# A one-core audio tower layer: the expert loop's engines hand over in rounds, with one signal per engine and step

## The chip, the cores and the metric

The kernel runs on one NeuronCore of a Trainium2 chip. The metric is device time in microseconds (us), the median over runs. Engines: PE (TensorE, matmuls and transposes), ACT (ScalarE), DVE (VectorE), POOL (GpSimd), SP (SyncE, which here only issues DMAs); the DMA engines move data beside them. Engines wait for each other with semaphores: an instruction may increment one at its end, and another engine waits until the count is reached. "Signal" below means such an increment.

## What is computed

The input is x, 128 x 125 x 64. A depthwise convolution of stride 2 (5 taps) with a group norm and PReLU gives 128 x 63 x 64; a selective state-space block and then a mixture of experts are added to it, each behind a layer norm. The change touches the experts:

```python
xf = x.reshape(-1, D)                       # 8064 tokens of 64
logits = xf @ Wr + br                       # 64 experts
topk_logits, topk_idx = jax.lax.top_k(logits, TOP_K)      # TOP_K = 2
gates = jax.nn.softmax(topk_logits, axis=1)
combine = jnp.zeros((T, E), xf.dtype).at[jnp.arange(T)[:, None], topk_idx].add(gates)
for e in range(E):
    h = jax.nn.relu(xf @ W1[e] + b1[e])     # 64 -> 128
    y = h @ W2[e] + b2[e]                   # 128 -> 64
    out = out + combine[:, e:e + 1] * y
```

All of it is float32.

## The kernel before, in words

The tokens lie as 63 tiles of 128. The first half of the program (to about 380 us) computes convolution and state-space block. Then the routing: DVE finds each token's two experts (`choose`, MAX8 and FIND_INDEX8 per tile), PE counts and ranks them, DVE works out for each token a row in a table sorted by expert. POOL scatters the tokens into this table, `sorted_rows`, with one indirect DMA per tile and choice (L629, 126 of them), and after the experts gathers their results from `expert_out` with 126 more (L650). The 63 tiles are dealt with in three shares (16, 24 and 23 tiles), each with tables of its own; a share's experts need all its scatters, its gathers all its experts' results.

**The expert loop** (about 514 to 778 us) has 80 steps. A step takes two pairs, a pair two tiles of 128 rows, each tile with the weights of one expert. In a step
- PE transposes the rows (`rows_T`, L886, 2 instructions), multiplies by W1 (`hidden`, L897, 8) and by W2 (`outputs`, L910, 8);
- ACT copies the transposes out of PSUM (`xT_copy`, L1165), takes the relu of one half of the hidden values (`relu_A`, L1174, 2), issues a load of rows every second step (L369), and stores the results of a step (`store`, L1183);
- DVE takes the other half's relu (`relu_B`, L1610, 2) and copies the outputs from PSUM into `y_e` (`y_copy`, L1620). Behind each copy it makes two pieces of the gates table (`gates_at`, L1629), and every eighth step adds eight tiles of it (L1637);
- SP loads the weights of a pair (L438) into a ring of 23 places as soon as the copy of the step that used the place is done.

The loop is written out, and each hand-over has a semaphore of its own: `s_rT` (transposes done), `s_rTc` (copied), `s_hid`, `s_reluA`, `s_reluB`, `s_yps` (outputs done), `s_yb` (copied). PE's order in step i is rows_T(i+2), hidden(i+1), outputs(i). All eight PSUM banks are in use; the outputs have one set (banks 6 and 7), so outputs(i) wait for y_copy(i-1). The outputs are computed for 192 columns, of which the last 64 are wanted: the weights lie as W1 (128 columns), W2 (64), bias (1) in a row, and columns 0 to 191 are multiplied.

POOL doesn't run freely in the loop. `keep_pace` makes every second indirect DMA wait until DVE has copied a given step: DMA number d (0 to 251, scatters and gathers together) waits for step (d - 56) * 80 / 153, for even d from 58 to 208. From d = 206 on the gathers are those of the last share, which need all stores. After the loop PE computes the bias part (transposes L942, matmuls L933), ACT and DVE pass it on (L1220, L1665), and DVE weights and adds the gathered rows (L1657, L1659).

DVE's helper `Chain` counts its own instructions on `s_dve`; `link` increments and waits.

## Time and profile before

| | |
|---|---|
| median of 3 runs | 859.83 us (858.7 to 861.21) |
| the profiled execution | 855.41 us |
| its span, first to last instruction | 853.5 us |
| granted TensorE clock, mean over the span | 0.826 of full speed |
| busy, share of the span | PE 60%, DVE 66%, ACT 39%, POOL 70% |
| instructions | 9083 |
| moved by DMA | 85 MB, 100 GB/s over the span |

The profile is one execution, so sums are made against its 855.41. An engine's busy time counts its working instructions; a PE instruction's end is modelled, and PE can be shown as done while the signal of its end is still to come. Releasers are inferred from the records of the semaphores; "remote" and "another core or an unknown queue" mean that no releaser was found, "issue" that the engine waited for nothing that the profile shows. The granted clock is 1.0 at 2.4 GHz and 0.5 at 1.2 GHz.

### The profile page before, as it was taken

To read this page: it belongs to the slowest core of one execution; us is meant where nothing else is said; L and a number is where in the kernel's file an instruction comes from. 1 tells how busy PE (TensorE), PEld (TensorE's weight loads), DVE (VectorE), ACT (ScalarE), POOL (GpSimd) and SP (SyncE) were. 2 spreads that over 40 slices of the span, in tenths; PEclk is the share of its full clock that TensorE was granted. 3 is DMA by queue.
4 is the path that set the end of the run, shared out by engine and by line. 5 is a ranking of instruction groups with operands and counts; after the bars stand their busy time and mean duration, and the time that the engine had idled before them with its cause. 6 is when DMAs were issued, how large, how long until landed. Compare 5 with 4: busy or idle time off the path is not lost.

```text
span 853.5 us, 9083 instructions
## 1 busy us (share of the span) xinstructions
PE 511.2 (60%) x2514; PEld 338.5 (40%) x2520; DVE 565.8 (66%) x1180; ACT 331.1 (39%) x622; POOL 600.2 (70%) x393
## 2 busy tenths in 40 slices
PE   4744245657568566556636767867677768786100
PEld 4733012222122222223323445756566657666100
DVE  1597899999999999997815763445444444332073
ACT  2159856556556655543311412323322332322000
POOL 5895779999999999991364454655555555564674
PEclk9969568797878789986756786999999998999655
DMA  7999950000000000000036013887877877831122
GB/s 247 383 180 123 74 3 0 0 0 0 0 1 0 0 0 0 0 0 0 20 84 161 15 67 110 229 222 211 235 225 209 241 214 208 224 90 47 23 73 62
DMA packets 106605, 84.96 MB, mean 100 GB/s; under 512 B 30464, under 2 KB 90240, under 8 KB 106560
## 3 DMA queue, kind: packets, MB, share of 16 engines
q1 hardware_dynamic: 79312, 54.76, 29.8%
q10 hardware_dynamic: 19184, 21.40, 8.0%
q0 software_dynamic: 8064, 8.27, 4.0%
q8 instruction: 19, 0.31, 0.2%
q14 instruction: 26, 0.21, 0.1%
HBM read 57.22 MB, written 33.49 MB: 106 GB/s over the span
## 4 chain that ended last, share of the span: by engine, by line
POOL 28%; PE 24%; DVE 16%; issue 14%; another core or an unknown queue 11%; ACT 4%; SPq 1%; POOLq 1%; DMA 0%; DVEq 0%; ACTq 0%
POOL x_w L577 14%; POOL w_ring L570 11%; PE ps L910 10%; PE ps L897 5%; POOL xt L650 3%; DVE x_w L1610 2%; DVE x_w L1620 2%; PE ps L675 2%; PE ps L739 1%; PE ps L886 1%; DVE mi L1515 1%; DVE lstat L1297 1%; PE ps L766 1%; PE ps L664 1%
## 5 line engine op out<-in xcount | busy, mean ns | idle before, releaser
L739 PE MATMUL ps<-x_w,ident 128*128 128x512 f32 x252 | 153.8, 770 | 100.7 <-POOL x_w L577 100.7
L629 POOL DMA_INDIRECT sorted_rows<-xp,slot_i x126 | 123.7, 981 | 116.4 <-DVE x_w L1620 35.2
L650 POOL DMA_INDIRECT xt<-expert_out,slot_i x126 | 123.3, 979 | 84.7 <-DVE x_w L1620 42.7
L570 POOL TENSOR_TENSOR w_ring<-xt,bc 128x2016 f32<-128x2016 f32 x32 | 143.4, 4483 | 13.4 <-DVE hh_ring L1426 7.3
L1426 DVE TENSOR_TENSOR_SCAN hh_ring<-ps,w_ring 128x1024 f32<-128x1024 f32 x64 | 147.5, 2305 | 0.1
L577 POOL TENSOR_TENSOR x_w<-hh_ring,bc 128x2016 f32<-128x2016 f32 (+1 forms) x32 | 141.1, 4411 | 1.2 <-PE ps L739 1.2
L739 PEld LDWEIGHTS ps<-x_w,ident 128*128 128x128 f32 x252 | 60.2, 249 | 197.0 <-POOL x_w L577 123.2
L1620 DVE COPY x_w<-ps 128x256 f32<-128x256 f32 x80 | 33.9, 424 | 108.0 <-remote 53.7
L1074 ACT ACTIVATE ps<-dt_t,a_exp 128x1024 f32<-128x1024 f32 x64 | 71.6, 1119 | 64.2 <-DVE hh_ring L1426 64.1
L1068 ACT ACTIVATE ps<-dt_t,a_exp 128x1024 f32<-128x1024 f32 x64 | 71.6, 1119 | 51.0 <-DVE w_ring L1405 51.0
L1165 ACT ACTIVATE x_w<-ps 128x256 f32<-128x256 f32 x80 | 30.8, 385 | 138.7 <-PE ps L886 57.6
L1405 DVE TENSOR_TENSOR w_ring<-ps,w_ring 128x1008 f32<-128x1008 f32 x64 | 78.3, 1223 | 4.1 <-ACT ps L1068 4.1
L1420 DVE SCALAR_TENSOR_TENSOR w_ring<-ps,w_ring 128x1008 f32<-128x1008 f32 x64 | 77.4, 1209 | 0.0
L910 PE MATMUL ps<-dt_t,x_w 128*128 128x192 f32 x280 | 57.2, 346 | 27.2 <-DVE x_w L1620 26.2
L910 PEld LDWEIGHTS ps<-dt_t,x_w 128*128 128x128 f32 x280 | 46.5, 195 | 32.2 <-issue 23.5
L910 PE MATMUL ps<-x_w 128*128 128x192 f32 x224 | 45.5, 345 | 17.6 <-DVE x_w L1620 13.5
L910 PEld LDWEIGHTS ps<-x_w 128*128 128x128 f32 x224 | 37.0, 194 | 21.5 <-issue 13.6
L910 PE MATMUL ps<-bc,x_w 128*128 128x192 f32 x136 | 28.7, 352 | 18.0 <-DVE x_w L1620 17.9
L1610 DVE TENSOR_SCALAR x_w<-ps,dt_t 128x128 f32<-128x128 f32 x70 | 21.5, 346 | 21.1 <-PE ps L897 19.2
L886 PE MATMUL ps<-ident,x_w 128*128 128x128 f32 x160 | 32.0, 285 | 0.4 <-issue 0.4
L910 PEld LDWEIGHTS ps<-bc,x_w 128*128 128x128 f32 x136 | 23.3, 200 | 20.7 <-issue 19.9
L1174 ACT ACTIVATE x_w<-ps,dt_t 128x128 f32<-128x128 f32 x70 | 22.2, 365 | 23.7 <-PE ps L897 20.4
(209 smaller groups left out, 887.9 us busy)
## 6 DMA issues: line engine op xcount, KB each, us to landing
dt_t<-packed SPq DMA_DIRECT2D x140, 96.5 KB
x_w<-packed SPq DMA_DIRECT2D x112, 96.5 KB
x_w<-sorted_rows ACTq DMA_DIRECT2D x40, 256.0 KB
expert_out<-x_w ACTq DMA_DIRECT2D x80, 128.0 KB
sorted_rows<-pad_rows SPq DMA_DIRECT2D x2, 3584.0 KB, 24.1
bc<-packed SPq DMA_DIRECT2D x68, 96.5 KB
packed<-in_L_ffn_W SPq DMA_DIRECT2D x3, 2048.0 KB, 42.0
x_w<-in_x SPq DMA_DIRECT2D x7, 448.0 KB, 8.7
```

What stands on the lines that cost most here:

```text
L570: pool.tensor_tensor(w_buf(k, 2), up3[:, bass.ds(c * DC, DC), 1:S].unsqueeze(1).broadcast_to([P, 2, DC, L]), vec_of(k, 2), ALU.mult).then_ ...
L577: pool.tensor_tensor(hc_buf(k, n), h_buf(k, n), vec_of(N + k, n), ALU.mult).then_inc(s_hcp, n)
L629: pool.indirect_dma_start(out=sorted_rows[h], out_offset=bass.IndirectOffsetOnAxis(ap=slot_i[:, c, l:l + 1], axis=0), in_=xn[:, l, :], in_ ...
L650: pool.indirect_dma_start(out=y[:, l, :], out_offset=None, in_=expert_out[h], in_offset=bass.IndirectOffsetOnAxis(ap=slot_i[:, c, l:l + 1] ...
L739: ins = pe.matmul(ps[:, i, :], ident[:, :], src[:, i * BANK:(i + 1) * BANK], start=(k < 0), stop=(k == (N - 2 if last else N - 1)), skip_g ...
L910: last = pe.matmul(ps[:, 6 + j, t * OUT:(t + 1) * OUT], hT_e[:, i % 2, t, j, :], w_of(n)[:, t, 0:OUT], start=True, stop=True)
L1068: act.activation(banks(6, 2), d, ACT.Tanh, scale=a_exp[:, 2, k:k + 1]).then_inc(s_th, 1)
L1074: act.activation(banks(2 + 2 * (k % 2), 2), d, ACT.Exp, scale=a_exp[:, 1, k:k + 1]).then_inc(s_dA, 1)
L1405: dve.tensor_tensor(wv, body(banks(6, 2)), wv, ALU.mult).then_inc(s_g, 1)
L1420: dve.scalar_tensor_tensor(out=wv, in0=body(dA), scalar=1.0, in1=wv, op0=ALU.add, op1=ALU.mult).then_inc(s_b, 1)
L1426: dve.tensor_tensor_scan(hh_ring[:, k % 4, :], dA, w_ring[:, k % 4, :], 0.0, ALU.mult, ALU.add).then_inc(s_h, 1)
L1620: dve.tensor_copy(y_e[:, i % YRING, 0:m], ps[:, 6:6 + m, 0:2 * OUT].rearrange("p q (t d) -> p q t d", d=OUT)[:, :, :, OUT - C:OUT]).then_i ...
```

## The change

The loop becomes rounds. In round k PE does outputs(k-4), hidden(k-2) and rows_T(k) and then increments one semaphore, `s_pstep`. ACT's round k waits for that and does xT_copy(k) and relu_A(k-2), then `s_astep`; behind it come the load of rows and store(k-5). DVE's round k waits for PE's round k and does relu_B(k-2) and y_copy(k-4), then `s_dstep`; behind it the gates of k-2. PE's round k waits for ACT's and DVE's rounds k-2. There are 84 rounds. The outputs of a step now fill one bank, alternately 6 and 7: four pieces of 128 columns (`OUT = 2 * C`), the last 64 wanted. SP and POOL wait for `s_dstep` where they waited for `s_yb` (`dve_rounds` turns a number of copied steps into one of rounds), and `LAG` grows from 12 to 16, so DMA d waits for step (d - 60) * 80 / 153, for even d from 62 to 212. Outside the loop DVE no longer increments after each instruction of a run of independent ones, only after the last.

```diff
+LAG_H, LATE = 2, 4
...
-OUT = 3 * C
+OUT = 2 * C
...
-LAG = 12
+LAG = 16
...
+def dve_rounds(steps):
+    return steps + LATE - LAG_H
...
                 if n >= WRING:
-                    sp.wait_ge(s_yb, step_of(n - WRING) + 1)
+                    sp.wait_ge(s_dstep, dve_rounds(step_of(n - WRING) + 1))
...
                 if d in STEP_AT:
-                    pool.wait_ge(s_yb, STEP_AT[d])
+                    pool.wait_ge(s_dstep, dve_rounds(STEP_AT[d]))
...
             def outputs(i):
 
-                pe.wait_ge(s_reluA, i + 1)
-                pe.wait_ge(s_reluB, i + 1)
-                if i >= 1:
-                    pe.wait_ge(s_yb, i)
                 for j, n in enumerate(pairs_of(i)):
                     for t in range(2):
-                        last = pe.matmul(ps[:, 6 + j, t * OUT:(t + 1) * OUT], hT_e[:, i % 2, t, j, :],
-                                         w_of(n)[:, t, 0:OUT], start=True, stop=True)
-                last.then_inc(s_yps, 1)
-
-            rows_T(0)
-            rows_T(1)
-            hidden(0)
-            for i in range(STEP0[-1]):
-                if i + 2 < STEP0[-1]:
-                    rows_T(i + 2)
-                if i + 1 < STEP0[-1]:
-                    hidden(i + 1)
-                outputs(i)
+                        last = pe.matmul(ps[:, 6 + i % 2, (2 * j + t) * OUT:(2 * j + t + 1) * OUT], hT_e[:, i % 2, t, j, :],
+                                         w_of(n)[:, t, HID + C - OUT:HID + C], start=True, stop=True)
+                return last
+
+            for k in range(STEP0[-1] + LATE):
+                if k >= LAG_H:
+                    pe.wait_ge(s_astep, k - LAG_H + 1)
+                if k >= LATE:
+                    pe.wait_ge(s_dstep, k - 2 * LAG_H + 1)
+                    last = outputs(k - LATE)
+                if LAG_H <= k < STEP0[-1] + LAG_H:
+                    last = hidden(k - LAG_H)
+                if k < STEP0[-1]:
+                    last = rows_T(k)
+                last.then_inc(s_pstep, 1)
...
+            for k in range(STEP0[-1] + LAG_H):
+                act.wait_ge(s_pstep, k + 1)
+                if k < STEP0[-1]:
+                    last = xT_copy(k)
+                if k >= LAG_H:
+                    last = relu_A(k - LAG_H)
+                last.then_inc(s_astep, 1)
+                if k < STEP0[-1]:
+                    next_rows(k)
+                if k > LATE:
+                    store(k - LATE - 1)
+            for i in range(STEP0[-1] + LAG_H - LATE - 1, STEP0[-1]):
+                store(i)
...
                 for l in range(v.start, v.stop):
-                    dve.max(mx[:, l, :], logits[:, l, :]).then_inc(s_dve, 1)
-                ch.at = ch.at + v.stop - v.start
-                dve.wait_ge(s_dve, ch.at)
+                    last = dve.max(mx[:, l, :], logits[:, l, :])
+                ch.link(last)
...
-            relu_B(0)
-            for i in range(STEP0[-1]):
-                if i + 1 < STEP0[-1]:
-                    relu_B(i + 1)
-                y_copy(i)
+            for k in range(LAG_H, STEP0[-1] + LATE):
+                dve.wait_ge(s_pstep, k + 1)
+                if k < STEP0[-1] + LAG_H:
+                    last = relu_B(k - LAG_H)
+                if k >= LATE:
+                    last = y_copy(k - LATE)
+                last.then_inc(s_dstep, 1)
+                i = k - LAG_H
```

**PE, two steps early in the loop.** `ps` is PSUM, `x_w` the memory with rows, hidden values and some of the weights, `dt_t` other weights; "x3" means three more like it. Before:

```order
L897 MATMUL ps<-x_w 128x128 [waits s_rTc,s_win5,s_win4]
L897 MATMUL ps<-x_w 128x128 x3
L910 MATMUL ps<-x_w 128x192 [waits s_yb,s_reluB,s_reluA]
L910 MATMUL ps<-x_w 128x192 x3
L886 MATMUL ps<-ident,x_w 128x128 [waits s_rows2]
L886 MATMUL ps<-ident,x_w 128x128
L897 MATMUL ps<-x_w 128x128 [waits s_rTc,s_win7,s_win6]
L897 MATMUL ps<-x_w 128x128 x3
```

Now, with `hidden` still L897, `outputs` L906 and the transposes L887:

```order
L906 MATMUL ps<-x_w 128x128 [waits s_dstep,s_astep]
L906 MATMUL ps<-x_w 128x128 x3
L897 MATMUL ps<-x_w 128x128 [waits s_win5,s_win4]
L897 MATMUL ps<-x_w 128x128 x3
L887 MATMUL ps<-ident,x_w 128x128 [waits s_rows2]
L887 MATMUL ps<-ident,x_w 128x128
L906 MATMUL ps<-x_w 128x128 [waits s_dstep,s_astep]
L906 MATMUL ps<-x_w 128x128 x3
```

The outputs stand first in a round and carry all its waits for other engines; hidden waits for its weights alone, and the outputs are 128 columns wide.

**DVE, a step in the loop.** `s_st0` and `s_st1` are the semaphores of the stores that must have landed before a place of `y_e` is written again. Before:

```order
L1620 COPY x_w<-ps 128x256 [waits s_yps,s_st0]
L1629 TENSOR_SCALAR us_lg<-iota_e,top 128x64
L1629 TENSOR_SCALAR hh_ring<-iota_e,top,gate 128x64
L1610 TENSOR_SCALAR x_w<-ps,dt_t 128x128 [waits s_hid]
L1610 TENSOR_SCALAR x_w<-ps,dt_t 128x128
L1620 COPY x_w<-ps 128x256 [waits s_yps,s_st1]
```

Now:

```order
L1595 TENSOR_SCALAR x_w<-ps,dt_t 128x128 [waits s_pstep]
L1595 TENSOR_SCALAR x_w<-ps,dt_t 128x128
L1604 COPY x_w<-ps 128x256 [waits s_st0]
L1612 TENSOR_SCALAR us_lg<-iota_e,top 128x64
L1612 TENSOR_SCALAR hh_ring<-iota_e,top,gate 128x64
L1595 TENSOR_SCALAR x_w<-ps,dt_t 128x128 [waits s_pstep]
```

The two relus and the copy of a round have one wait for PE, ahead of the relus; before, relus and copy had one each. The copy is of a step two before that of the relus; it was one before.

## Rows read from the trace of the kernel before

**Rows 1.** The page, the chain that ended last, by engine.
```profile
POOL 28%; PE 24%; DVE 16%; issue 14%; another core or an unknown queue 11%; ACT 4%; SPq 1%; POOLq 1%; DMA 0%; DVEq 0%; ACTq 0%
```

**Rows 2.** By stretch: PE, PEld, DVE, ACT, POOL busy, clock, DMA share, GB/s.
```profile
560.00:600.00 40.00, 30.57 (x233) 26.25 (x232) 17.97 (x63) 12.44 (x38) 23.65 (x24) 1.00 0.80 223
```

**Rows 3.** Waits, 520 to 780 us: us in total, times, longest.
```profile
ACT x_w L1165 <- PE ps L886: 57.6, 37, 4.3
...
DVE x_w L1620 <- remote: 53.7, 25, 4.5
```

**Rows 4.** Timeline, 630.5 to 638.5: start, us, instructions, [idle before <-releaser].
```profile
630.74 0.42 DVE L1620 COPY x_w<-ps 128x256 f32<-128x256 f32 x1 [2.34 <-remote]
...
631.44 1.01 POOL L629 DMA_INDIRECT sorted_rows<-xp,slot_i  x1 [1.66 <-DVE x_w L1620]
...
632.69 0.38 PE L886 MATMUL ps<-ident,x_w 128*128 128x128 f32 x2
...
633.10 0.39 ACT L1165 ACTIVATE x_w<-ps 128x256 f32<-128x256 f32 x1 [1.49 <-PE ps L886]
...
633.64 1.57 PE L910 MATMUL ps<-x_w 128*128 128x192 f32 x8
...
635.30 0.97 POOL L629 DMA_INDIRECT sorted_rows<-xp,slot_i  x1 [0.30 <-issue]
...
637.25 0.38 ACT L1165 ACTIVATE x_w<-ps 128x256 f32<-128x256 f32 x1 [2.33 <-remote]
637.28 0.42 DVE L1620 COPY x_w<-ps 128x256 f32<-128x256 f32 x1 [2.37 <-remote]
...
637.85 1.54 PE L910 MATMUL ps<-x_w 128*128 128x192 f32 x8 [1.77 <-DVE x_w L1620]
```

**Rows 5.** Timeline: first wait in the loop, first gather after it, bias part.
```profile
524.84 1.01 POOL L629 DMA_INDIRECT sorted_rows<-xp,slot_i  x1 [7.04 <-DVE x_w L1620]
...
780.99 0.95 POOL L650 DMA_INDIRECT xt<-expert_out,slot_i  x1 [6.76 <-DMA expert_out<-x_w]
...
809.35 0.69 DVE L1665 TENSOR_TENSOR hg<-ps,hg 128x512 f32<-128x512 f32 x1 [15.50 <-remote]
```

**Rows 6.** Timeline, 638 to 648: a run of six indirect DMAs.
```profile
638.52 0.99 POOL L650 DMA_INDIRECT xt<-expert_out,slot_i  x1 [2.25 <-DVE x_w L1620]
...
640.18 1.57 PE L910 MATMUL ps<-x_w 128*128 128x192 f32 x8
...
642.93 0.42 DVE L1620 COPY x_w<-ps 128x256 f32<-128x256 f32 x1 [2.02 <-PE ps L910]
...
644.93 0.95 POOL L650 DMA_INDIRECT xt<-expert_out,slot_i  x1 [0.30 <-issue]
...
647.24 0.61 DVE L1610 TENSOR_SCALAR x_w<-ps,dt_t 128x128 f32<-128x128 f32 x2 [3.44 <-PE ps L897]
```

**Rows 7.** Groups, POOL, 520 to 780: busy us, mean ns | idle before <-releasers.
```profile
L650 POOL DMA_INDIRECT xt<-expert_out,slot_i x80 | 77.2, 966 | 60.7 <-DVE x_w L1620 42.7 <-issue 18.1
L629 POOL DMA_INDIRECT sorted_rows<-xp,slot_i x68 | 67.2, 989 | 51.2 <-DVE x_w L1620 35.2 <-issue 16.1
```

**Rows 8.** Timeline: outputs at half clock, bias matmuls; then stretches as in rows 2.
```profile
521.21 2.90 PE L910 MATMUL ps<-x_w 128*128 128x192 f32 x8 [3.19 <-DVE x_w L1610]
...
782.60 1.06 PE L933 MATMUL ps<-b2w,w_ring 128*128 128x128 f32 x8
...
520.00:524.00 4.00, 2.79 (x9) 2.74 (x10) 1.12 (x4) 1.42 (x5) 0.00 (x0) 0.50 0.00 0
...
645.00:648.00 3.00, 0.91 (x11) 0.55 (x9) 0.76 (x3) 0.76 (x3) 0.89 (x1) 0.98 0.55 139
648.00:651.00 3.00, 2.67 (x8) 2.63 (x9) 1.14 (x5) 0.77 (x3) 1.96 (x2) 0.50 0.84 217
651.00:655.00 4.00, 4.00 (x32) 3.34 (x31) 2.69 (x9) 1.40 (x4) 2.36 (x3) 0.97 0.82 231
```

**Rows 9.** The chain in order of time: DVE's statistics of 16 tiles.
```profile
409.40 2.03 DVE lstat L1458 x16
```

More of the change, by code:

```diff
@@ L331, in build @@
         s_win = [sem(f"s_win{k}") for k in range(WRING)]
[L332 to L338 removed]
+        s_pstep = sem("s_pstep")
+        s_astep = sem("s_astep")
+        s_dstep = sem("s_dstep")
         s_st = [sem(f"s_st{k}") for k in range(YRING)]
@@ L887, in rows_T @@
                                         ident[:, :])
-                last.then_inc(s_rT, 1)
+                return last
             def hidden(i):
@@ L1201, in _ @@
                 rows_of_unit(v)
-            for i in range(2):
-                xT_copy(i)
-                next_rows(i)
-            relu_A(0)
-            for i in range(STEP0[-1]):
-                if i + 2 < STEP0[-1]:
-                    xT_copy(i + 2)
-                    next_rows(i + 2)
-                if i + 1 < STEP0[-1]:
-                    relu_A(i + 1)
-                if i > 0:
-                    store(i - 1)
-            store(STEP0[-1] - 1)
+            for k in range(STEP0[-1] + LAG_H):
[11 more added lines that the diff above has]
+                store(i)
             for q in range(CQ):
@@ L1457, in positions_of @@
                 for l in range(a, z):
-                    dve.bn_stats(lstat[:, l, :], hg[:, l, :]).then_inc(s_dve, 1)
-                ch.at = ch.at + z - a
+                    last = dve.bn_stats(lstat[:, l, :], hg[:, l, :])
+                last.then_inc(s_dve, 1)
+                ch.at = ch.at + 1
             def variance_of(c):
@@ L1510, in choose @@
                 for l in range(v.start, v.stop):
[L1511 to L1513 removed]
+                    last = dve.max(mx[:, l, :], logits[:, l, :])
+                ch.link(last)
                 for l in range(v.start, v.stop):
[L1515 to L1517 removed]
+                    last = dve.max_index(mi[:, l, :], mx[:, l, :], logits[:, l, :])
+                ch.link(last)
                 ch.link(dve.tensor_copy(top[:, 2:4, v], mi[:, v, 0:2].rearrange("p l c -> p c l")))
@@ L1611, in relu_B @@
                                              w_of(n)[:, 1, HID + C:WROW], 0.0, ALU.add, ALU.max)
-                last.then_inc(s_reluB, 1)
+                return last
             def y_copy(i):
@@ L1628, in gates_at @@
                 for k in range(2):
-                    dve.tensor_scalar(comb[k][:, l, :], iota_e[:, :], top[:, 2 + k, l:l + 1], gates[k][:, l:l + 1],
-                                      ALU.is_equal, ALU.mult).then_inc(s_dve, 1)
-                ch.at = ch.at + 2
+                    last = dve.tensor_scalar(comb[k][:, l, :], iota_e[:, :], top[:, 2 + k, l:l + 1], gates[k][:, l:l + 1],
+                                             ALU.is_equal, ALU.mult)
+                if l % 8 == 7 or l + 1 == L:
+                    last.then_inc(s_dve, 1)
+                    ch.at = ch.at + 1
             def both_gates(q):
@@ L1641, in _ @@
                 ch.link(dve.memset(comb[k][:, L, :], 0.0))
-            relu_B(0)
-            for i in range(STEP0[-1]):
-                if i + 1 < STEP0[-1]:
-                    relu_B(i + 1)
-                y_copy(i)
+            for k in range(LAG_H, STEP0[-1] + LATE):
[6 more added lines that the diff above has]
+                i = k - LAG_H
                 if i > 0 and i % 8 == 0 and i // 8 <= CQ:
```

50 lines of the change are left out of this document (13 added, 37 removed).

## The prediction

> **What bounds the kernel now.** The span is 853.5 us, and the chain of waits that ends last has no single owner: POOL 28%, PE 24%, DVE 16%, "issue" 14%, and 11% "another core or an unknown queue" [rows 1]. On one core the last is a signal whose way the profile can't name, so the stretch that it stands in must be read by hand. That stretch is the expert loop, about 514 to 778 us. In a 40 us window of it PE is busy 30.6 us at the full granted clock, DVE 18, ACT 12.4, POOL 23.7, and the DMA engines 80% [rows 2]: nothing is full. The waits say what stops them: ACT waits 57.6 us for transposes and DVE 53.7 us for a "remote" releaser [rows 3], although PE is not late.
>
> The timeline shows why. POOL's indirect DMAs take 0.97 us and follow each other with 0.30 us between. POOL restarts at 631.44 once DVE's copy of 630.74 is done. The transposes that PE starts at 632.69 and ends at 633.07 reach ACT at 633.10, at once. But the outputs of 633.64 end at 635.21 and the copy that waits for them starts at 637.28, and ACT's copy of the next transposes at 637.25, both "remote" [rows 4]. What happened between is that POOL stopped, at 635.30 + 0.97 = 636.27. **PE's signals are held back while POOL issues indirect DMAs, once its run is some 2 us old, and come through about 1 us after it stops.** The hold can be long: behind the loop, where POOL isn't paced, DVE waited 15.50 us for one [rows 5]. Inside a run a signal gets through now and then, one at a time: outputs that ended at 641.75, 3.2 us into a run, reached DVE at 642.93 with POOL still running, while the hidden layers of the same run waited until 647.24, 1.4 us after its end at 645.88 [rows 6].
>
> So the loop is POOL's. From 517.8 to 774.3 it issues 148 DMAs: 144.4 us busy, 34.2 us of forced 0.3 us gaps, 77.9 us in 38 waits for DVE's copies [rows 7]. The first wait is 7.04 us [rows 5]; the other 37 take 70.9 us, 1.92 us each. Pacing grants 153 DMAs per 80 steps, so 37 waits over 75 steps mean one hole every two steps: four DMAs, a stop, about 1 us until the signals come, copy, restart. That is the period, about 6.6 us. A step's own PE work is 640.18 - 637.85 = 2.33 us [rows 4, 6], 4.7 of it for two steps.
>
> **The change, part by part.**
> *Rounds.* PE sends one signal per step in place of three, and in round k waits only for what ACT and DVE did in round k-2. So at the end of a hole PE has two rounds done, k-1 and k, and both signals are waiting. DVE takes them one behind the other, and POOL and PE restart after the first. Each hole is then dearer. It was 1.92 us. It becomes 0.98 (POOL's end to the signal, 636.27 to 637.25) + 0.61 (both relus, which now stand ahead of the copy) + 0.42 (copy) + 0.28 (631.16, the copy's end, to POOL's 631.44) = 2.29 us, call it 2.3 [rows 4, 6].
> *How many steps a hole now serves.* Rounds k-1 and k come for certain. Round k+1 starts with POOL's restart and, at 1.8 us (next item), ends in the first 2 us of the run, when signals pass. Round k+2 ends about 3.7 us into it. No row shows a lone signal there. The nearest: one 3.2 us in came through with 1.1 us delay [rows 6]; one 3.8 us in did not [rows 4], but there a signal of hidden had to go ahead of it, and that is the kind that goes. Between 3 steps (it never passes) and 5 (it and the next pass) I take 4. Holes cost 2.3 x 75/4 = 19 holes, 43.7 us; each hole that vanishes still costs the 0.3 us gap, 18 x 0.3 = 5.4. Against 70.9 us: **-21.8 us**. The ends: 3 steps give 25 holes, 57.5 + 3.6, so -9.8; 5 steps give 15, 34.5 + 6.6, so -29.8; no holes at all leave 37 x 0.3, so -59.8.
> *Outputs 128 columns wide, not 192.* Eight bias matmuls of 128x128 with 128 columns take 1.06 us, the outputs now 1.57 us [rows 4, 8]. So PE's round falls from 2.33 to 1.82 us. On its own this is worth nothing: PE waits for signals, not they for PE. Its worth is in putting round k+1 into the free 2 us.
> *PSUM two deep* takes the wait for the copy one step before out of PE's way; it is the condition of the rounds and counted there. *ACT's store* of step k-5 waits for DVE's round k-1, and the next round's transposes and relus are queued behind it; PE wants them two rounds later, and DVE's round is 0.6 + 0.42 + two gates, so I cost it at nothing. If the hold were gone it would come next, with PE's 1.82.
> *SP and POOL* wait for rounds in place of copies. The copy of a step now comes in round k+4, two rounds later against the row loads than before; POOL's LAG grows by 4 DMAs, which is two steps. Weight loads are asked for some ten rounds ahead, still over 25 us. The first wait moves from DMA 58 to DMA 62: four DMAs more (5.1 us) run first, and the first hole, now 7.0, should be 1 to 2 us shorter; at the end POOL waits for four trailing rounds, 1 to 4 us more than the present 6.8 [rows 5]. Together 0, within 4 us either way.
> *DVE's runs signal with their last.* Sixteen statistics start in 2.03 us, 127 ns apart, signals and all [rows 9]; nothing there waits for a signal of its own before the run's end. Between 0 and, if each of some 190 short instructions in the routing part gave 10 ns, -2 us: I take 0, since none of these waits was found behind an increment.
> *DMA.* At 80% and 223 GB/s [rows 2] the same bytes in a loop 22 us shorter (of 256) mean 88%: still under full, and part of why I don't go for the ends without holes.
>
> **Sum:** the profiled execution took 855.4 us (span 853.5), the median of the runs is 4.4 above it. 859.8 - 21.8 = **838 us**.
>
> The Trainium skill has a rule for the price of an increment: in "TensorE: Matmul & The Clock Gate", section "The cost: per-tile semaphore tail", increments on matmuls serialize at 26.3 ns each. By it the 160 increments fewer would be worth 4.2 us, and the time would be 855.6. The holds of 2 us and 15.5 us [rows 4, 5] are far from such a price, so the trace speaks against it as the whole story.
>
> **The rivals.**
> *(B) The signals flow.* If what clogs the way is the number of signals, three per step, then with one the hold may be nearly gone, and the loop runs at POOL's own 1.27 us per DMA. For: within a run one signal at a time does pass. Against: behind the loop, where few signals are sent, one was held for 15.5 us. Time: -30 to -60, 800 to 830 us. 0.15.
> *(C) Nothing that matters changes:* holes come as rarely as makes up for their price. 2.3 H + 0.3 (37 - H) = 70.9 gives H = 30, 2.5 steps per hole: no change, 857 to 862. 0.06. This is also where it would land if only the increments' own cost went away.
> *(D) Slower: two steps per hole, through the clock.* A hole still serves two rounds, as now, if round k+1 ends later than 2 us into POOL's run. At 1.8 us there are 0.2 us to spare at the full clock and none at the half clock, where the eight outputs of 521.21 took 2.90 us in place of 1.57 [rows 8]. And the change takes work from PE: two rounds of 1.8 in a period of 7.1 are 51% busy, with an idle piece of 3 us. The granted clock was 1.00 (2.4 GHz) while PE was busy 3/4 of the time [rows 2]; in 645 to 648, with 0.91 us of work in 3, it fell, and 648 to 651 ran at 0.50, 1.2 GHz, before 651 to 655 was back at 0.97 [rows 8]. Decided by whether k+1's signal passes: then 37.5 holes at 2.3 are 86.3 against 70.9, +15, so 875; with part of the rounds at half clock, up to 890. For: the idle pieces do get longer. Against: in a slow round PE is busy again, and that brought the clock back within 3 us. 0.25. The same page of the Trainium skill, under "HAM oscillation", says that pauses between bursts of matmuls send the clock back to half; 645 to 651 agrees.
>
> **How the numbers follow.** Forecast (3 to 5 steps per hole, 826 to 854 with the 4 us of the ends): 0.54. B 0.15, C 0.06, D 0.25. The measurement of this kernel can tell 0.3%, 2.6 us. Faster 0.69 (forecast and B), same 0.06, slower 0.25. The range leaves out about a tenth at each end: 806, inside B, to 872, inside D. The forecast's own range is 826 to 854.
>
> **What would show it.** Right: POOL's waits for DVE between 517 and 775 fall from 38 to about 20, each 2.2 to 2.4 us; runs of 6 to 10 DMAs; copies start in pairs 1.6 us apart behind a hole, the next single; outputs take 1.06 us. A POOL wait total near 50 us. Wrong: about 37 waits of 2.3 us and a PE clock at 0.5 over tens of us (D); POOL waiting under 20 us in all (B), or a loop in which PE or ACT waits for weights or rows, which would make the DMA engines the bound. The part behind the loop, 46 gathers from 780.99 on, should stay at 72.5 us; a difference there is none of my terms.

## The result and the profile after

The changed kernel took 863.2 us (median of 12 runs, 860.2 to 865.3), the kernel before 859.2 us on the same chip (12 runs, 855.0 to 863.3). The ratio of the two is 1.0055, 95% interval 1.0035 to 1.0074: **slower by a little over half a per cent**, where 838 us and faster was forecast. The profiled execution took 861.9 us, its span is 859.9.

The time can be read on POOL, as in the prediction. First the waits of POOL in the changed kernel's loop (engine, line, releaser; us in total, times, longest):

```profile
POOL sorted_rows L630 <- DVE x_w L1604: 35.4, 11, 9.1
POOL xt L651 <- DVE x_w L1604: 32.3, 14, 4.0
POOL xt L651 <- issue: 20.4, 67, 0.3
POOL xt L651 <- DMA expert_out<-x_w: 19.0, 2, 10.8
POOL sorted_rows L630 <- issue: 17.8, 57, 0.7
```

A "hole" below is such a pause of POOL's, a "run of POOL's" the indirect DMAs between two holes. Against the waits of before [rows 5, 7]: the waits for DVE's copies fell from 38 of 77.9 us to 25 of 67.7. The waits for stores (`expert_out`) were 6.8 us and are 19.0; a further wait at the same place, 2.6 us before, was counted with DVE's. Sorted by place, POOL's idle time changed so: without the first wait and the two places of the stores there were 36 holes of 68.3 us and are 24 of 58.6, 9.7 us less; all shorter gaps together grew by 3.6, mostly since each hole that vanishes leaves a forced one; the first wait grew by 2.0, the two store waits together by 9.7 (9.3 to 19.0). That adds up to the 5.6 us by which the loop is longer: from the end of POOL's 58th indirect DMA to the first gather of the last share it was 263.2 us and is 268.8. The part behind the loop was 72.5 and is 73.5, and so the spans differ by 6.4 us.

One period of the changed loop, out of the timeline (start, duration, engine, line, what it works on, idle time before it and its releaser; weight loads, ACT, DMA queues, DVE's gates and some rows of POOL and PE are left out). It answers to [rows 4, 6]:

```profile
587.06 0.44 PE L887 MATMUL ps<-ident,x_w 128*128 128x128 f32 x2
588.46 0.97 POOL L630 DMA_INDIRECT sorted_rows<-xp,slot_i  x1 [0.30 <-issue]
588.97 0.44 PE L887 MATMUL ps<-ident,x_w 128*128 128x128 f32 x2
590.80 0.35 DVE L1595 TENSOR_SCALAR x_w<-ps,dt_t 128x128 f32<-128x128 f32 x1 [4.32 <-PE ps L887]
591.33 0.41 DVE L1604 COPY x_w<-ps 128x256 f32<-128x256 f32 x1
591.89 0.68 PE L906 MATMUL ps<-dt_t,x_w 128*128 128x128 f32 x4 [2.49 <-DVE x_w L1604]
592.02 1.01 POOL L630 DMA_INDIRECT sorted_rows<-xp,slot_i  x1 [2.59 <-DVE x_w L1604]
592.62 0.42 DVE L1604 COPY x_w<-ps 128x256 f32<-128x256 f32 x1
594.12 0.69 PE L887 MATMUL ps<-ident,x_w 128*128 128x128 f32 x2
594.60 1.86 PE L906 MATMUL ps<-bc,x_w 128*128 128x128 f32 x8
594.85 0.61 DVE L1595 TENSOR_SCALAR x_w<-ps,bc 128x128 f32<-128x128 f32 x2 [1.36 <-PE ps L887]
597.04 0.44 PE L887 MATMUL ps<-ident,x_w 128*128 128x128 f32 x2
597.32 1.06 PE L906 MATMUL ps<-bc,x_w 128*128 128x128 f32 x8
598.46 0.97 POOL L630 DMA_INDIRECT sorted_rows<-xp,slot_i  x1 [0.30 <-issue]
598.95 0.44 PE L887 MATMUL ps<-ident,x_w 128*128 128x128 f32 x2
600.78 0.35 DVE L1595 TENSOR_SCALAR x_w<-ps,x_w 128x128 f32<-128x128 f32 x1 [4.54 <-PE ps L887]
```

POOL stops at 589.43. PE's rounds that ended with its transposes of 587.06 and 588.97 are seen by DVE together, the first at 590.80. POOL restarts at 592.02, after a hole of 2.59 us. The next round of PE starts at 591.89. The granted clock falls to 0.50 at 592.87 and is back at 1.00 at 596.28, so its hidden layers take 1.23 us in place of 0.72. It ends at 594.81, 2.8 us into POOL's run, and its signal passes at once (594.85). The one after it ends at 597.48, 5.5 us into the run, and is not seen before 600.78. So a hole serves **three steps**, six DMAs, in a period of about 10.0 us; before it was two in 6.6.

The clock, with the busy time of PE, PEld, DVE, ACT and POOL, then granted clock, DMA share and GB/s, in windows of 40 us:

```profile
560.00:600.00 40.00, 30.01 (x216) 25.49 (x216) 16.89 (x61) 10.53 (x36) 23.48 (x24) 0.83 0.75 213
600.00:640.00 40.00, 28.70 (x216) 24.14 (x216) 18.51 (x66) 11.48 (x40) 21.88 (x22) 0.87 0.80 221
```

It was 1.00 [rows 2]. PE stands idle for 2.5 us in the hole shown, and parts of the two rounds behind it run at half clock: the eight outputs of 594.60 take 1.86 us, those of 597.32 take 1.06.

At the end of the second share POOL waits for stores that now come behind two more rounds, and then runs without pause:

```profile
691.59 0.95 POOL L651 DMA_INDIRECT xt<-expert_out,slot_i  x1 [0.30 <-issue]
700.72 0.95 POOL L651 DMA_INDIRECT xt<-expert_out,slot_i  x1 [8.18 <-DMA expert_out<-x_w]
...
717.08 0.95 POOL L651 DMA_INDIRECT xt<-expert_out,slot_i  x1 [0.30 <-issue]
```

While POOL is silent here, the copies come every 1.91 us. In the run of 14 DMAs that follows there is a gap of 15.8 us between two copies.

### The profile page after: what moved, and what is told of

Same layout as the page of the kernel before. It is cut to its first block, busy times and chain, and to the rows that moved or that the text cites. A ratio compares the mean times of both kernels' runs of the same rounds, so it can differ in the third digit from the quotient of the medians.

```text
span 859.9 us, 8932 instructions
## 1 busy us (share of the span) xinstructions
PE 512.3 (60%) x2514; PEld 334.2 (39%) x2520; DVE 561.7 (65%) x1180; ACT 323.0 (38%) x622; POOL 599.8 (70%) x393
## 4 chain that ended last, share of the span: by engine, by line
PE 29%; POOL 21%; DVE 18%; issue 12%; another core or an unknown queue 10%; ACT 7%; SPq 1%; POOLq 0%; DMA 0%; ACTq 0%; DVEq 0%
POOL w_ring L571 9%; POOL x_w L578 9%; PE ps L906 9%; PE ps L897 6%; PE ps L887 5%; DVE hh_ring L1419 4%; DVE x_w L1595 2%; PE ps L740 2%; POOL xt L651 2%; PE ps L676 2%; ACT ps L1072 2%; DVE x_w L1604 1%; DVE mi L1507 1%; DVE lstat L1290 1%
## 5 line engine op out<-in xcount | busy, mean ns | idle before, releaser
L740 PE MATMUL ps<-x_w,ident 128*128 128x512 f32 x252 | 162.1, 804 | 92.5 <-POOL x_w L578 92.5
L740 PEld LDWEIGHTS ps<-x_w,ident 128*128 128x128 f32 x252 | 62.7, 259 | 194.5 <-POOL x_w L578 116.9
L906 PE MATMUL ps<-dt_t,x_w 128*128 128x128 f32 x280 | 46.9, 319 | 29.7 <-DVE x_w L1604 29.2
L1595 DVE TENSOR_SCALAR x_w<-ps,x_w 128x128 f32<-128x128 f32 x56 | 17.3, 346 | 66.7 <-remote 37.0
L906 PE MATMUL ps<-x_w 128*128 128x128 f32 x224 | 37.9, 321 | 33.0 <-DVE x_w L1604 23.9
L906 PEld LDWEIGHTS ps<-dt_t,x_w 128*128 128x128 f32 x280 | 42.5, 231 | 32.3 <-ACT x_w L1167 31.5
L906 PEld LDWEIGHTS ps<-x_w 128*128 128x128 f32 x224 | 34.4, 233 | 35.5 <-ACT x_w L1167 33.8
L887 PE MATMUL ps<-ident,x_w 128*128 128x128 f32 x160 | 40.8, 343 | 1.5 <-issue 1.5
L740 PE MATMUL ps<-hh_ring,ident 128*128 128x512 f32 x16 | 11.1, 832 | 33.2 <-ACT hh_ring L1055 26.0
L897 PE MATMUL ps<-x_w,dt_t 64*128 64x128 f32 x280 | 30.2, 339 | 0.0
```

Source lines behind the costliest of these rows:

```text
L740: ins = pe.matmul(ps[:, i, :], ident[:, :], src[:, i * BANK:(i + 1) * BANK], start=(k < 0), stop=(k == (N - 2 if last else N - 1)), skip_g ...
L887: last = pe.transpose(ps[:, i % 2, j * P:(j + 1) * P], rows_in[:, u % RING, in_share(n) % UNIT, :], ident[:, :])
L897: last = pe.matmul(ps[:, 2 + 2 * (i % 2) + t, j * P:(j + 1) * P], w_of(n)[t * C:(t + 1) * C, t, 0:HID], xT_e[t * C:(t + 1) * C, i % 2, j, ...
L906: last = pe.matmul(ps[:, 6 + i % 2, (2 * j + t) * OUT:(2 * j + t + 1) * OUT], hT_e[:, i % 2, t, j, :], w_of(n)[:, t, HID + C - OUT:HID + C ...
```

## The experiments

There were 18 further runs. The kernel before ran beside each, and one thing has to be known first: **the chips differ**. The comparisons came in seven groups, each on one chip: in four of them before takes 853 to 859 us, in three, on two other chips, 757 to 759. I call them chips that hold (PE's signals) and chips that don't, for the reason shown under 3. Every ratio is against before on the same chip.

### 1. The parts alone (a chip that holds, before 854.4 us)

`e_dve` is before with DVE's new signals only: in the layer norm's statistics, in `choose`, in the rows of the sorted table and in the gates. `e_width` is before with the narrow outputs only:

```diff
-OUT = 3 * C
+OUT = 2 * C
-                                         w_of(n)[:, t, 0:OUT], start=True, stop=True)
+                                         w_of(n)[:, t, HID + C - OUT:HID + C], start=True, stop=True)
```

> The kernel before with one part of the change alone: DVE's runs in the routing part and its gates signal with their last. Nothing waits for an increment inside these runs. The prediction's step (no gain, at most -2 us): within 0.3% of before, 857 to 862. Rival, each increment costs DVE time that is on the path: 3 to 6 us less than before.

Measured: 856.3 us, ratio 1.0007 (0.9968 to 1.0046). No gain is visible, as predicted; the interval doesn't exclude 2 us.

> The kernel before with the outputs 128 columns wide in place of 192, nothing else. PE's step falls from 2.33 to 1.82 us. Theory H (PE's signals are held while POOL issues indirect DMAs, and the rhythm is set by the holes): worth nothing, within 0.3% of before, still one hole per two steps (38 waits of POOL for DVE). Rival K (the clock): less PE work means more idle PE, the granted clock in the loop falls from 0.96 to 1.00 to below 0.9 and the loop gets slower by 3 us or more, as it did in the changed kernel.

Measured: 850.6 us, ratio **0.9932** (0.9892 to 0.9972), and in a repeat on another chip that holds

> The kernel before with outputs 128 wide, as in the run e_width. Where before takes about 757: if the changed kernel's 0.7% there comes from PE's shorter step, this gives the same 0.7%; if from the rounds, it gives nothing. Where before takes about 855: 0.7% again, as in e_width, against the +0.55% of the changed kernel, so that the rounds themselves cost 1.2%.

850.3 against 853.4, 0.9956 (0.9919 to 0.9993). So the width alone is worth 0.4 to 0.7%, where the expectation of `e_width` had nothing or a loss. POOL's waits in the loop of `e_width`:

```profile
POOL xt L650 <- DVE x_w L1620: 33.9, 17, 3.6
POOL sorted_rows L629 <- DVE x_w L1620: 30.5, 16, 5.9
POOL xt L650 <- issue: 21.8, 65, 1.0
POOL sorted_rows L629 <- issue: 17.7, 53, 0.8
POOL xt L650 <- DMA expert_out<-x_w: 5.5, 1, 5.5
```

The 33 waits for copies look like fewer holes than the 38 of before, but seven pauses of 0.5 to 1.0 us stand under "issue" here. Counted by length, POOL pauses for over 0.5 us 41 times in `e_width` and 41 in the first profile of before, and on another chip 44 times in `r_width` and 40 in `r_before`; runs of six DMAs are not more frequent either (6 and 2, against 5 and 8). So a hole doesn't serve more steps. What is shorter is the idle time: between POOL's 58th and 207th DMA 108.5 us, against 117.6 in `e_dve` on the same chip, and 108.0 against 113.6 in the other pair. Of these 9.1 and 5.6 us the two places of the stores give 5.5 and 2.6, the first wait 0.8 and 0.9, and the rest comes from the holes and gaps between. The granted clock was 0.91 in three windows of the loop, where `e_dve` on the same chip has 0.91, 0.96 and 0.96: a little lower, with a gain all the same.

Set beside the changed kernel, this tells what the rounds do. These are two profiles from different chips, one execution each, and the changed kernel also has DVE's new signals and the larger `LAG`. Without the first wait (9.1 us with rounds, 5.9 here) it is 24 holes of 2.44 us, 58.6 us, against 32 waits of 1.83, 58.5 us, and the shorter gaps come to 37.7 and 37.9 us. **Fewer and dearer holes cancel.** What is left is the later first copy, 3.1 us, and the later stores, 19.0 us at both places against 6.2: 15.9 us, and the loops, counted from the start of the 58th DMA, differ by 16.1 (269.8 and 253.7 us). In the medians the difference is smaller, 1.1% or some 10 us.

### 2. POOL silent in the second part of the loop (same chip)

```diff
-                    pool.wait_ge(s_st[j], 16 * ((STEP0[h + 1] + YRING - 1 - j) // YRING))
+                    pool.wait_ge(s_st[j], 16 * ((STEP0[-1] + YRING - 1 - j) // YRING))
```

> The kernel before with the gathers of all three shares behind the last share's stores, so that POOL is silent from its 126th indirect DMA to the end of the loop, and 126 gathers in place of 46 run behind it. Theory H: in the silent part no signal of PE is held, the loop is PE's own, 2.3 us per step, and the total is near 922 us (46 steps of 2.33, then 126 gathers of 1.27). Rival N (the hold comes from the number of PE's signals, three per step): holds and waits for a remote releaser go on in the silent part, over 3 us per step, total over 950.

> The changed kernel with the same edit. Theory H: 1.9 us per step in the silent part, which is PE's round at the full clock, no delay between the end of PE's round and ACT's copy, total near 906 us, 16 below the same edit on the kernel before. Rival K (in the changed kernel the idle PE at half clock sets the pace): 2.7 us per step in the silent part too, total near 940. Rival N: no difference from theory H here, one signal per step flows.

Measured, one execution each: 918.3 and 908.5 us, 10 us apart where 16 were expected. The copies mostly come every 2.4 us and every 1.9 us once POOL is silent. Windows of 40 us of the second, with POOL at work and without:

```profile
600.00:640.00 40.00, 29.39 (x224) 24.89 (x223) 18.10 (x67) 11.49 (x39) 21.31 (x22) 0.84 0.83 235
640.00:680.00 40.00, 40.00 (x377) 34.82 (x376) 29.75 (x106) 18.03 (x61) 0.00 (x0) 0.99 0.95 280
```

and one signal of the silent part:

```profile
660.41 0.44 PE L887 MATMUL ps<-ident,x_w 128*128 128x128 f32 x2
...
660.88 0.38 ACT L1162 ACTIVATE x_w<-ps 128x256 f32<-128x256 f32 x1 [1.01 <-PE ps L887]
```

PE is busy 40.00 us of 40 at a clock of 0.99. All 43 rounds that end in the silent part release ACT and DVE 0.04 us later, and in the kernel before none of the 127 signals with records there is more than 0.03 us late, although there are three per step. The DMA engines are busier in the silent part shown (a share of 0.95) than with POOL at work (0.83). So it is POOL's indirect DMAs that hold PE's signals, and not the number of signals: rival N is out. DVE's and ACT's signals aren't held: in the loops of before and of the changed kernel, with POOL at work, none of their recorded signals was more than 0.012 us late. The half clock is a consequence of the holes, not the pace.

### 3. Chips that don't hold

The next four runs, the two here and `e_narrow` and `e_d3` of section 5, fell on a chip where before takes 756.6 us.

> The changed kernel with ACT's store of step k-5 put ahead of ACT's wait for round k, in place of behind round k's work. Theory S (the late stores at the ends of the shares cost the 12 us by which the gain of fewer holes was eaten): waits for stores before DMAs 158 and 206 fall from 19.0 to about 11 us, the total by 5 to 8. Rival: it is the two trailing rounds themselves that are late, not the store behind them: within 2 us of the changed kernel.

```diff
             for k in range(STEP0[-1] + LAG_H):
+                if k > LATE:
+                    store(k - LATE - 1)
                 act.wait_ge(s_pstep, k + 1)
...
-                if k > LATE:
-                    store(k - LATE - 1)
```

> The changed kernel, but POOL's pacing waits for PE's round (k+1 signals of PE) instead of DVE's. The hole loses DVE's relus and copy: 1.3 us in place of 2.6. Theory H3 with the 2 us of free signals: PE starts its next round only 1.0 us after POOL restarts, which now ends 2.9 us or more into the run and is held, so a hole serves 2 steps: four DMAs, 37 holes of 1.3 us, 48 us of waits in place of 68, and 18 us less in all (845 where before is 859). Rival: the next round's signal still passes, 3 steps per hole, 25 holes of 1.3: 33 us less. Rival: the shorter pause lets no signals through, or only one: slower.

```diff
-                    pool.wait_ge(s_dstep, dve_rounds(STEP_AT[d]))
+                    pool.wait_ge(s_pstep, STEP_AT[d] + LATE)
```

752.6 us (0.994, 0.992 to 0.996) and 752.0 us (0.994, 0.991 to 0.997). Neither tests its theory, because nothing waits there. To see this I ran the changed kernel and `e_pace` again; they fell on a second chip of that kind, before 758.7 us:

> The changed kernel again, beside the kernel before, since the last four runs were on a chip on which the kernel before takes 757 us and POOL never waits. Theory H with chips that differ (some hold PE's signals while POOL issues indirect DMAs, others do not): on a chip where before takes about 855, the ratio is 1.005 as at first; on a chip where before takes about 757, the loop is POOL's own string of DMAs in both kernels, ratio 0.99 to 1.00. Rival: the four runs were fast through their edits (not possible for all, since before itself was fast there).

> POOL's pacing by PE's rounds in place of DVE's, as in the run e_pace. On a chip that holds signals, theory H3 with its free first 2 us: two steps per hole, 37 holes of 1.3 us, some 18 us less than the changed kernel. Rival: 3 steps per hole of 1.3 us, 33 less. On a chip that holds none: the same as the changed kernel within 3 us.

`r_after` took 752.1 us, ratio **0.9928** (0.9900 to 0.9956), `r_pace` 753.2 us (0.994, 0.991 to 0.996). On such a chip the change is a gain of 0.7%. POOL's waits in the loop of `r_after`, and one window:

```profile
POOL xt L651 <- issue: 23.8, 78, 0.3
POOL sorted_rows L630 <- issue: 19.5, 64, 0.3
POOL xt L651 <- DVE x_w L1604: 1.5, 5, 0.3
```

```profile
560.00:600.00 40.00, 32.13 (x292) 27.80 (x288) 23.93 (x85) 14.43 (x48) 30.24 (x33) 0.96 1.01 300
```

No hole is left. All 79 of PE's rounds that end while POOL works in the loop release ACT or DVE within 0.05 us, with POOL never stopping; the loop is POOL's 149 DMAs of 1.27 us, 188.7 us in place of 269.8, and the DMA engines are full at 300 GB/s. The same kernel differs by 110 us between two chips: 81 in the loop, 5 behind it, and 23 ahead of it, where POOL's 58th DMA starts at 493.1 in place of 516.6. Up to POOL's first indirect DMA the two executions run alike (it starts at 418.0 and 418.5 us), so the whole difference arises once POOL issues them. What makes the chips differ stays open. Whether the gain of 0.7% comes from the width, the rounds or DVE's signals there is open too: `r_before` and `r_width` were meant for it and fell on a chip that holds.

> The kernel before, for its profile on this chip. If the chip is one on which it takes about 757 us: no delay between a signal of PE and its waiter while POOL issues indirect DMAs, few or no waits of POOL for DVE in the expert loop, DMA 58 to 206 in about 190 us; a step of PE 2.3 to 2.4 us, just under POOL's own 2.43 per step. If it is one of about 855 us: the holes of 1.9 us as in the first profile.

853.5 us, and 40 pauses of POOL over 0.5 us in the loop, where the first profile has 41.

### 4. The pacing by PE's rounds, on chips that hold

> POOL's pacing by PE's rounds in place of DVE's, once more. On a chip that holds signals, theory H3 with its free first 2 us: two steps per hole, 37 holes of 1.3 us, some 18 us less than the changed kernel. Rival: 3 steps per hole of 1.3 us, 33 less. On a chip that holds none: within 3 us of the changed kernel.

Measured: 839.1 us against 853.4, ratio **0.9865** (0.9807 to 0.9923), 1.9% below the changed kernel's 1.0055, which comes from another chip. The rhythm is as expected, four DMAs and mostly some 1.25 us:

```profile
597.84 0.97 POOL L630 DMA_INDIRECT sorted_rows<-xp,slot_i  x1 [1.28 <-PE ps L887]
...
601.65 0.97 POOL L630 DMA_INDIRECT sorted_rows<-xp,slot_i  x1 [0.30 <-issue]
603.88 0.97 POOL L630 DMA_INDIRECT sorted_rows<-xp,slot_i  x1 [1.26 <-PE ps L887]
605.15 0.98 POOL L630 DMA_INDIRECT sorted_rows<-xp,slot_i  x1 [0.30 <-issue]
```

```profile
POOL sorted_rows L630 <- PE ps L887: 23.8, 16, 5.1
POOL xt L651 <- PE ps L887: 20.5, 15, 2.0
...
POOL xt L651 <- DMA expert_out<-x_w: 18.3, 2, 10.6
...
POOL xt L651 <- remote: 3.2, 1, 3.2
POOL sorted_rows L630 <- remote: 1.2, 1, 1.2
```

31 waits of 44.3 us, and two of 4.4 us whose releaser the profile doesn't name, where the changed kernel has 25 of 67.7. PE's next round now starts 0.8 us behind POOL's restart and mostly ends 3.0 us into the run. Of the 17 rounds that ended 2.75 to 3.25 us into one, none came through at once and 14 were held beyond its end, so a hole mostly serves two steps. The moment alone isn't the rule, though: in the changed kernel 13 of 15 rounds that ended 2.75 to 3.75 us into a run came through at once (ACT and DVE started 0.04 us later), and all 36 that ended later were held beyond the run's end. What lets a signal through in that stretch stays open.

> The changed kernel with POOL's pacing by PE's rounds (as in e_pace) and LAG 12 in place of 16, so that POOL stands two steps further behind the loop when it comes to the stores of a share. On a chip that holds signals: still two rounds and 1.25 us per hole; the waits for stores before DMAs 158 and 206, 10.6 and 7.7 us in r_pace2, become 3 to 4 us shorter each, the first wait 2 us longer; in all 4 us less than r_pace2 (839 where before is 853: 835). Rival: the time spent there is not lost, since the rounds that pass in it are saved later: within 2 us of r_pace2. On a chip that holds none: within 4 us of the changed kernel.

Measured: 837.4 us against 857.5 on another chip that holds, ratio **0.978** (0.975 to 0.981). In its profile the waits for stores are 12.3 us in place of 18.3. But the first wait is 2.4 us longer, the other holes are 36 of 48.9 us in place of 32 of 43.5 (pauses over 0.5 us, whatever their releaser), and the loop is 245.5 us in place of 244.5. So in the two profiles what the stores save comes back as holes, as the rival says. The times leave it open: in us `e_p12` is 1.6 faster, within the rival's 2, but before was 4 us slower on its chip, and by the ratios it is 0.85% better, some 7 us. It has the lowest ratio of all on chips that hold, 2.7% below the changed kernel's if the two are set side by side.

### 5. Deeper rounds and narrower outputs

```diff
-OUT = 2 * C
+OUT = C
```

> The changed kernel with the outputs 64 columns wide in place of 128, nothing else. PE's round at half clock falls from 2.71 to about 2.1 us. Theory H3 (a hole of POOL serves LAG_H + 1 = 3 rounds, whatever their length: the two that stand finished, and the next one): still six DMAs per hole, 2.6 us each, within 3 us of the changed kernel (863 where before is 859). Rival K (the length of PE's round decides, since at half clock the round k+2 ends too late in POOL's run): some holes serve 4 steps, eight DMAs between them, and the time falls by 8 us or more.

Measured: 831.2 to 835.0 us in five executions and 813.5 in the sixth, where before takes 756.6: **7.5 to 10% slower**. A window of the loop in the profiled execution, which took 835.0 us, and one round:

```profile
600.00:640.00 40.00, 40.00 (x218) 35.90 (x214) 17.23 (x61) 10.78 (x36) 23.29 (x25) 0.50 0.81 213
```

```profile
570.27 0.69 PE L887 MATMUL ps<-ident,x_w 128*128 128x128 f32 x2
570.75 1.80 PE L906 MATMUL ps<-x_w 128*128 128x64 f32 x8
572.48 1.23 PE L897 MATMUL ps<-x_w 64*128 64x128 f32 x8
```

PE is busy without a break and is granted 0.50, 1.2 GHz, from one end of the loop to the other. Its round takes 3.4 us, and POOL waits for it. The execution of 813.5 us had a mean granted clock of 0.713 over its span, the other five 0.679 to 0.683; how its loop ran isn't on record. Neither theory had this.

`e_d3` makes the rounds three deep. Each of the three steps in work gets two of the eight PSUM banks: one with the transposes and the first hidden layer (both read by ACT), one with the outputs and the second (both read by DVE). That needs outputs of 64 columns.

```diff
-LAG_H, LATE = 2, 4
+LAG_H, LATE = 3, 6
-                    last = pe.transpose(ps[:, i % 2, j * P:(j + 1) * P],
+                    last = pe.transpose(ps[:, 2 * (i % LAG_H), j * P:(j + 1) * P],
```

> The changed kernel with rounds three deep in place of two (LAG_H 3, LATE 6, buffers three deep, outputs 64 wide so that they share banks, y ring of six, LAG 20). Theory H3: each hole serves 4 steps, eight DMAs between holes, so about 19 holes of 2.7 us in place of 25 of 2.6: 14 us less; the waits for the stores at the ends of the shares grow by two rounds each (2 x 3.8 us). In all 4 to 10 us less than the changed kernel. Rival K or C (something else than the number of finished rounds sets the rhythm): still six DMAs per hole, time 5 us or more above the changed kernel.

833.8 to 839.9 us in five executions and 812.9 in the sixth, beside 756.6. The profile (836.3 us) has the same half clock (0.50, 3.4 us per round), so it says nothing of the depth. `e_d3f` adds work for PE behind each signal, in banks that nobody reads:

```diff
                 last.then_inc(s_pstep, 1)
+                for j in range(3):
+                    pe.matmul(ps[:, 6 + k % 2, j * P:(j + 1) * P], ident[:, :], ident[:, :], start=True, stop=True)
```

> The changed kernel with rounds three deep (LAG_H 3, LATE 6, outputs 64 wide, LAG 20) and three matmuls of 128 columns behind each round's signal, into banks that nobody reads, which keep PE as busy as the outputs of 128 columns do. Rival K for the run e_narrow (outputs 64 wide leave PE too little work, and it runs at half clock for good): the granted clock is back at 0.8 or more, and PE's round below 2.4 us. On a chip that holds no signals: then within 5 us of the changed kernel. On one that holds them, theory H3: four steps per hole, eight DMAs between holes, 4 to 10 us less than the changed kernel; rival: still six.

On a chip that holds: 875.6 us against 853.4, 1.026 (1.020 to 1.032). The clock is back (0.87 to 0.92 in the loop), but PE's round is 2.5 us, over the 2.4 asked for, and of POOL's 30 runs in the loop 13 have six DMAs, 14 have two or four and one has eight: mostly three steps per hole or fewer, not four. PE is busy up to 37.1 us of 40, so with rounds of 2.5 us there was hardly room for a fourth. Theory H3, depth plus one, isn't borne out.

> The changed kernel with rounds three deep, POOL's pacing by PE's rounds, LAG 16 (as late as LAG 12 at depth two), outputs 64 wide and one matmul of 128 columns behind each round's signal for the clock, so that PE's round is about 2.0 us in place of the 2.5 of e_d3f. On a chip that holds signals, theory H4 (a hole serves as many rounds as stand finished when POOL stops, which is the depth, plus what ends in the first 3 us of POOL's run): three rounds, six DMAs, 1.25 us per hole: 25 holes instead of 37, 15 us less in holes and 4 to 8 more at the shares' ends, so 825 to 835 where before is 853. Rival: the depth does not matter, PE gets no third round done within the run: 840 or more. On a chip that holds none: within 5 us of the changed kernel, if the granted clock stays over 0.75; at half clock for good, some 830, as e_narrow.

One such matmul in place of three, and the pacing of section 4: 905.8 us against 857.5, 1.056 (1.054 to 1.058), on a chip that holds. The clock was 0.50 again, the round 3.8 us. With three extra matmuls per round the windows show 0.87 to 0.92, with one 0.50.

> The run e_d3f (rounds three deep, three matmuls behind each round for the clock, a round of PE of 2.5 us) with POOL's pacing by PE's rounds and LAG 16. On a chip that holds signals, theory H4: three rounds stand finished at each hole, so six DMAs per hole and 1.3 us: a period of 8.9 us, in which PE's 7.6 us fit; 25 holes; the waits at the ends of the shares 6 to 8 us longer than e_p12's. In all within 8 us of e_p12, 0.97 to 0.985 of before, and the rhythm of six DMAs is what tells. Rival: four DMAs per hole as at depth two, 0.99 or more. Rival K: the clock falls to half for good as in e_d3gp, 1.05.

> The run e_p12 (pacing by PE's rounds, LAG 12) with PE's round started earlier: ACT signals its copy of the transposes by itself, and PE's next transposes stand first in its round and wait for that alone, before outputs and hidden. In r_pace2 the round after a hole ends 3.0 us into POOL's run and its signal is held to the end; here it would end about 2.5 us into it. On a chip that holds signals, theory H4: it passes (in the changed kernel rounds that ended 2.8 us into a run did), so a hole serves 3 steps: six DMAs and 1.3 us, 25 holes instead of 37, 12 to 15 us less than e_p12 (0.963 of before). Rival: the one more signal per round, or a hold that begins at 2 us, leaves two rounds per hole: within 3 us of e_p12 (0.978). On a chip that holds none: within 4 us of the changed kernel, 0.993.

```diff
                 if k >= LAG_H:
-                    pe.wait_ge(s_astep, k - LAG_H + 1)
+                    pe.wait_ge(s_xstep, min(k - LAG_H + 1, STEP0[-1]))
+                if k < STEP0[-1]:
+                    last = rows_T(k)
                 if k >= LATE:
+                    pe.wait_ge(s_astep, k - 2 * LAG_H + 1)
```

This is PE's part of `e_split`; ACT increments the new `s_xstep` behind its copy, and `s_astep` still behind its relus. Both fell on a chip that doesn't hold (before 757.9 us): 772.6 us, 1.018 (1.014 to 1.022), for `e_d3fp`, whose PE round of 2.5 us is now longer than POOL's 2.43 per step, and 754.5 us, 0.996 (0.993 to 0.999), for `e_split`. On the question of depth against moment they say nothing; it stays open. So does the pacing by PE's own signal without the rounds, which no run has.

## Why the prediction was wrong

**The mechanism stood.** PE's signals are held while POOL issues indirect DMAs and mostly come 1.0 to 1.4 us after it stops; with POOL silent none is late (section 2). But it belongs to the chip. One profile couldn't show that on others nothing is held, the loop is POOL's string and the change a gain of 0.7%. What failed is the account of what a hole costs and serves. The forecast was 838 us and the kernel took 863.2; that this lies between the 806 and 872 named as the outer ends is no merit of the forecast, since the upper end stands in rival D, two steps per hole, which didn't occur either.

**The step that failed is the number of steps per hole.** I took 4 (3 to 5), with the round k+1 at 1.8 us and k+2 ending 3.7 us into the run, and it was 3. In the period shown round k+1 took 2.92 us (591.89 to 594.81), part of it at half clock behind the idle piece; k+2 ended at 5.5 us and was late, as were all that ended later than 3.75 us. The full clock wouldn't clearly have saved it: in four of POOL's runs k+2 ended 3.9 to 4.2 us in, and it was held in all four. That half clock was rival D's mechanism, with half of its effect: k+1's signal passed all the same, at 2.8 us, where I had put the limit at 2. Had 3 steps been the only miss, my own sum would have given 850.

**The price of a hole** was put at 2.3 us and was 2.6: DVE saw the signal 1.37 us after POOL's stop (589.43 to 590.80), not 0.98. With 3 steps and that price my own sum gives 25 x 2.6 = 65 us, plus 3.6 of gaps, against 70.9: 2 us of gain, not 21.8. In the profile it is 24 holes of 58.6 us against 36 of 68.3 at the same places, 9.7 less, and 3.6 more of gaps: 6 us of gain, since the mean hole is 2.44 us and some steps pass at the stores' waits. (My 70.9 us held the 2.6 us of a store's wait.)

**The ends** were put at 0, within 4 us, and cost some 12: the first wait became 2.0 us longer, not 1 to 2 shorter, and the waits for stores 9.7 us longer in front of the second and the last share's gathers together (19.0 against 6.8 + 2.55). I had looked at the last share only, where 1 to 4 us more were forecast and 4.0 came, and had not asked what two more rounds do where POOL waits for the share before. In `e_p12` these waits were 6.0 us shorter than in `r_pace2` and the holes 5.4 us longer, so the 12 us overlap with the gain from fewer holes. `e_store` was to test the later stores and fell on a chip where nothing waits for them.

**The width** was "worth nothing" on its own and is the only part of the change that is seen to help on a chip that holds: 0.4 to 0.7%. The reason given for it, one more step inside the free part of a run, isn't what the profiles show: the pauses are as many as before. They, the first wait and the waits for stores are shorter, so "PE waits for signals, not they for PE" isn't true at every place. The rest of the change, above all the rounds, costs about 1.1% on such chips if ratios of different chips are set side by side (1.0055 against 0.993 and 0.996).

**Right:** DVE's increments are worth nothing that can be seen. The outputs take 1.06 us at the full clock. The part behind the loop changed by 1.0 us. The DMA engines stayed at about 80%, not 88, as the loop didn't get shorter. Rival B fell on this chip. Of the Trainium skill's price for an increment ("TensorE: Matmul & The Clock Gate", "The cost: per-tile semaphore tail"), an estimate of 4.2 us for 160 of them, the kernel with fewer shows nothing on a chip that holds: it is 1.1% above the one with the same width and all of them. Rival C comes nearest: holes as rare as makes up for their price. It had 6 chances in 100 and was worked out at 2.5 steps; at a price of 2.6 us its own equation gives 26 holes, 2.9 steps each.

## What to carry to other kernels

If an engine's waiters see its signals late while another issues indirect DMAs, count what a pause of that issuer costs and how many steps it releases, and try first to make the pause shorter: here moving the issuer's pacing from the end of the waiters' chain to the held signal itself gave 1.9 to 2.7% on top of the batched signals (ratios of different chips), while batching alone only traded the number of pauses for their length. When work is delayed by rounds, look at every place that waits for the last item of a group, not at the last group alone. And measure on more than one chip before a rhythm is taken for the kernel's own.

## What was not expected of the hardware

- The hold is there in four of seven groups of runs and absent in three, on two other chips. The same program, the changed kernel, took 863 us on one kind and 752 on the other; before took 853 to 859 and 757 to 759. Where the hold is absent, the DMA engines are full (share 1.01, 300 GB/s) in the same loop.
- With outputs of 128x64 in place of 128x128 TensorE stayed at the half clock for the whole loop of the profiled execution, with PE busy 40.00 us of 40. With 128 columns the loop's first window shows 0.96 on the same kind of chip, with PE busy 32.1 us of 40. The Trainium skill, in "TensorE: Matmul & The Clock Gate" under "HAM oscillation", puts the half clock down to pauses between bursts; the windows of `e_narrow` have no pause and the half clock nevertheless.
- On a chip that holds, a signal of PE's that ends 3 us into POOL's run came at once in one kernel (13 of 15, 2.75 to 3.75 us into the run) and never in another (0 of 17, 2.75 to 3.25 us), with the same round of PE.
- DVE's and ACT's recorded signals were at most 0.012 us late in the same loops in which PE's were up to 11.3 us late.
